# Whole-precision inverse products, DMA-transposed rows for the middle pairs, and the first norm's scaling at the end of beat 9

## The reference

```
u   = x @ in_proj_w.T + in_proj_b                # 512 -> 1536
uc  = short convolution of u, 3 taps, causal     # per channel, plus short_b
x0, x1, v = split(uc, 3)
k   = filter made by a small sine network, times a decay
v   = fftconv(v * x1, k) + bias * (v * x1)       # long causal convolution over 512 steps
x   = layernorm(x + (v * x0) @ out_proj_w.T + out_proj_b)
gate, up = x @ Wg.T, x @ Wu.T                    # 512 -> 1408; W = (codes - 128) * scale
x   = layernorm(x + (silu(gate) * up) @ Wd.T)
```

## Time and profile before

| | |
|---|---|
| median of 3 runs | 1064.79 us (1064.36 to 1066.73) |
| the profiled execution's own time | 1063.65 us |
| its span, first to last instruction | 1061.5 us |
| PE busy | 1023.4 us, 96% of the span, 6394 instructions |
| PEld busy | 831.9 us, 78% |
| DVE busy | 781.3 us, 74% |
| POOL busy | 639.2 us, 60% |
| ACT busy | 461.2 us, 43% |
| DMA queue q1, share of 16 engines | 27.2% |

### The profile page before, as it was taken

How to read it: one execution, slowest core, us unless ns; L and a number is a source line. 1 busy time by engine, 2 the same in 40 slices (tenths; PEclk the granted TensorE clock), 3 DMA queues, 4 the chain that set the end, 5 groups by cost and what they waited for, 6 DMA issues and landing times.

```text
span 1061.5 us, 18026 instructions
## 1 busy us (share of the span) xinstructions
PE 1023.4 (96%) x6394; PEld 831.9 (78%) x6394; DVE 781.3 (74%) x1416; ACT 461.2 (43%) x986; POOL 639.2 (60%) x685
## 2 busy tenths in 40 slices
PE   7998799999999999999999999999999999989996
PEld 5577678888888888888888888888888888868774
DVE  6577776877788787777878777787877778775554
ACT  4565344434454443444444444544435444424242
POOL 4578765675757567475756747575674756585210
PEclk9898899999999999999999999999999999999998
DMA  7565202222221312321122222312121212222232
GB/s 233 179 189 186 73 22 70 90 80 61 80 90 41 100 41 80 95 85 50 52 93 76 80 61 80 90 47 93 41 82 59 80 52 64 75 60 81 91 103 75
DMA packets 51783, 89.66 MB, mean 84 GB/s; under 512 B 6314, under 2 KB 11178, under 8 KB 51694
## 3 DMA queue, kind: packets, MB, share of 16 engines
q1 hardware_dynamic: 50930, 88.25, 27.2%
q10 hardware_dynamic: 764, 0.27, 0.1%
HBM read 77.22 MB, written 11.27 MB: 83 GB/s over the span
## 4 chain that ended last, share of the span: by engine, by line
PE 81%; DVE 7%; issue 4%; ACT 3%; POOL 2%; DMA 1%; ACTq 0%; SPq 0%; POOLq 0%; DVEq 0%
PE gate_up L995 12%; PE gate_up L996 12%; PE bank L852 10%; PE bank L854 10%; PE bank L853 10%; PE down L1006 7%; PE down L1007 7%; PE bank L956 3%; PE bank L978 1%; PE spectrum L852 1%; PE spectrum L854 1%; PE spectrum L853 1%; DVE tmp L755 1%; PE bank L909 1%; PE bank L957 1%
## 5 line engine op out<-in xcount | busy, mean ns | idle before, releaser
L602 ACT ACTIVATE hid<-gate_up,gate_scale 128x256 f32<-128x256 f32 x176 | 83.2, 473 | 208.3 <-PE gate_up L996 204.1
L755 DVE TENSOR_TENSOR tmp<-spectrum,filt 128x512 f32<-128x512 f32 x256 | 172.7, 679 | 0.0
L637 POOL TENSOR_TENSOR acc<-acc,tmp 128x256 f32<-128x256 f32 x160 | 124.4, 778 | 78.4 <-DVE tmp L755 68.1
L995 PE MATMUL gate_up<-x2T_hi,wg_sb 128*128 128x256 f16 x704 | 165.1, 275 | 0.0
L996 PE MATMUL gate_up<-x2T_lo,wu_sb 128*128 128x256 f16 x704 | 163.3, 273 | 0.0
L996 PE MATMUL gate_up<-x2T_lo,wg_sb 128*128 128x256 f16 x704 | 163.3, 273 | 0.0
L995 PE MATMUL gate_up<-x2T_hi,wu_sb 128*128 128x256 f16 x704 | 163.2, 273 | 0.0
L852 PE MATMUL bank<-xT_hi,win_hi 128*128 128x512 f32 x360 | 150.2, 417 | 2.9 <-POOL win_lo L620 1.7
L1006 PE MATMUL down<-wd_sb,hid_hi 128*128 128x512 f32 x352 | 147.8, 420 | 4.3 <-DVE hid_lo L842 2.2
L854 PE MATMUL bank<-xT_hi,win_lo 128*128 128x512 f32 x360 | 144.0, 400 | 0.0
L853 PE MATMUL bank<-xT_lo,win_hi 128*128 128x512 f32 x360 | 144.0, 400 | 0.0
(11 more groups left out here) (170 smaller groups left out, 2177.7 us busy)
## 6 DMA issues: line engine op xcount, KB each, us to landing
wd_sb<-wd_scratch SPq DMA_DIRECT2D x176, 256.0 KB, 2.6
xstage<-in_x SPq DMA_DIRECT2D x32, 256.0 KB, 4.3
x<-in_x SPq DMA_DIRECT2D x28, 256.0 KB, 2.7
out<-x SPq DMA_DIRECT2D x28, 256.0 KB, 3.3
x<-in_win SPq DMA_DIRECT2D x12, 256.0 KB, 4.8
acc<-in_decay SPq DMA_DIRECT2D x4, 256.0 KB
x<-in_wout SPq DMA_DIRECT2D x4, 256.0 KB, 2.8
x2T_hi<-in_wu SPq DMA_DIRECT2D x4, 256.0 KB, 4.1
```

Of the source, the lines that this page charges most:

```text
L637: G.tensor_tensor(acc[:, i, 0, :], acc[:, i, 0, :], t[:, 1, :], ALU.subtract)
L755: TT(dst, spectrum[j % 2][:, :, :], k_part, ALU.mult).then_inc(made_done, 1)
L995: mm(dst, w[:, kb, rows(q)], x2T_hi[:, kb, ts], start=kb == 0, stop=False)
```

## The change

It does four things.

1. All halves take the whole sums: `psplit`, `acc_hi`, `acc_lo`, `y_low`, `WHOLE` and `LIGHT` are gone, and `iv` is 4 calls of `matmul` on float32 for each of the four blocks of each half. `y` is one operation. The inverse matrix is no longer split, so one of 18 staged weights goes.
2. Pairs 1 to 12 (`BY_DMA`) have no `x2t` on PE. At the end of beat 10 ACT writes a float16 copy of each scaled row tile to `parts`, DVE writes the float16 rest, and SP issues four transposing DMAs (128x512 float16 each) to `x2T_hi` and `x2T_lo`. `gu` of unit 0 waits for all four. Pairs 0, 13, 14 and 15 keep `x2t`.
3. `norm` of LN1 stands at the end of beat 9 instead of near the start of beat 10.
4. `bank_read` becomes one semaphore for each bank, and an entry waits for the last read of its own bank.

```diff
-NFLOAT, NCODE, CODE_SLOTS = 18, 35, 5
+NFLOAT, NCODE, CODE_SLOTS, TEMPS = 17, 35, 5, 4
+BY_DMA = range(1, HALVES - 3)
-    if beat == 0 and 0 <= n - 3 < HALVES:
+    if beat == 0 and 0 <= n - 3 < HALVES and n - 3 not in BY_DMA:
         steps += [("x2t", n - 3, 0), ("x2t", n - 3, 1)]
-    if beat == 10 and out:
-        steps += [("norm", LN1, n - 2)]
+    if beat == 9 and out:
+        steps += [("norm", LN1, n - 2)]
     if beat in (9, 10):
         steps += readers([p for p in shared(n, beat) if p[0] == "xt"])
-    if beat in SPLIT_OF_BEAT and convs and n - 1 not in LIGHT:
-        steps += [("psplit", n - 1, SPLIT_OF_BEAT[beat])]
+    if beat == 10 and n - 2 in BY_DMA:
+        steps += [("x2part", n - 2, 0), ("x2part", n - 2, 1), ("x2dma", n - 2)]
...
+def by_dma(m):
+    return min(max(m - BY_DMA[0], 0), len(BY_DMA))
...
# SP
+elif kind == "x2dma":
+    m, = at
...
+    if m >= 2:
+        sp.wait_ge(gate_up_ready, HB * (m - 1))
+    for part, dst, done in ((0, x2T_hi, x2_hi_done), (1, x2T_lo, x2_lo_done)):
+        for b in range(2):
+            sp.wait_ge(done, 2 * (m if part == 0 else by_dma(m)) + b + 1)
+            sp.dma_start_transpose(dst[:, :, rows(pair_block(m, b))], parts[:, b, part, :]).then_inc(x2t_in, 16)
# ACT
+elif kind == "x2part":
+    m, b = at
+    act.wait_ge(ln_done[LN1], 2 * m + b + 1)
+    if m > BY_DMA[0]:
+        act.wait_ge(x2t_in, 64 * by_dma(m))
+    A(parts[:, b, 0, :], row_tile(m, b), ACT.Copy).then_inc(x2_hi_done, 1)
# DVE
+elif kind == "x2part":
+    m, b = at
+    dve.wait_ge(x2_hi_done, 2 * m + b + 1)
+    TT(parts[:, b, 1, :], row_tile(m, b), parts[:, b, 0, :], ALU.subtract).then_inc(x2_lo_done, 1)
# DVE, first product of a block
-                        if n - 1 in WHOLE:
+                        if n:
                             dve.wait_ge(bank_ready, use["iv", n - 1, i] + 1)
-                        elif n:
-                            dve.wait_ge(acc_lo_done, splits["psplit", n - 1, i] + 1)
# PE, iv
+                    pe.wait_ge(temp_added, temp["mul", n, i, i, 1] + 1)
+                    if k == use["iv", 0, 0]:
                         pe.wait_ge(inv_in, 16)
                     for c in range(2):
                         for r in range(2):
+                            last = mm(dst[:, rows(c)], acc[:, i, r, rows(c)], inv_sb[:, r, :], start=r == 0, stop=r == 1)
# PE, gu
-                    if q == 0:
-                        pe.wait_ge(bank_read, use["x2t", m, 1] + 1)
+                    if q == 0 and m in BY_DMA:
+                        pe.wait_ge(x2t_in, 64 * by_dma(m + 1))
+                    elif q == 0:
+                        pe.wait_ge(*read_of(use["x2t", m, 1]))
```

More of the change, by code:

```diff
@@ L203, in program @@
             now = beat_steps(n, beat)
-            at = next((k for k, s in enumerate(now) if s[0] in ("psplit", "mul")), len(now)) if n in (1, 2) else len(now)
+            at = next((k for k, s in enumerate(now) if s[0] == "mul"), len(now)) if n in (1, 2) else len(now)
             steps += now[:at] + setup_steps(n, beat) + now[at:]
@@ L257, in build @@
         acc = sb("acc", [P, TB, 2, W], F32)
-        acc_hi, acc_lo = (sb(f"acc_{n}", [P, 2, 2, W], F32R) for n in ("hi", "lo"))
-        tmp = sb("tmp", [P, 4, 2, W], F32)
+        tmp = sb("tmp", [P, TEMPS, 2, W], F32)
         za_hi, za_lo = (sb(f"za_{n}", [P, 2, L], F32R) for n in ("hi", "lo"))
@@ L264, in build @@
         hid = sb("hid", [P, 2, W], F32)
-        y_low = sb("y_low", [P, 2, P], F32)
+        parts = sb("parts", [P, 2, 2, D], F16)
         hid_hi, hid_lo = (sb(f"hid_{n}", [P, 2, W], F32R) for n in ("hi", "lo"))
@@ L295, in build @@
         gate_up_ready, down_done = sem("gate_up_ready"), sem("down_done")
-        bank_read, made_done = sem("bank_read"), sem("made_done")
+        bank_read, made_done = [sem(f"bank_read{n}") for n in range(4)], sem("made_done")
         temp_added = sem("temp_added")
@@ L367, in build, with last_use, read_of @@
         wide_ring = [bank[0][:, :], bank[1][:, :], flat(gate_up[0][:, :, :]), flat(gate_up[1][:, :, :])]
-        wide_uses = use["x2t", 0, 0] // 4 * 4
+        wide_uses = use["x2t", 0, 0]
+        bank_index = [k % 4 if k < wide_uses else (k - wide_uses) % 2 for k in range(len(use))]
         def bank_of(k):
-            return wide_ring[k % 4] if k < wide_uses else bank[k % 2][:, :]
+            return wide_ring[bank_index[k]]
+        def last_use(index, k):
+            return max((n for n in range(k) if bank_index[n] == index), default=None)
+        def read_of(k):
+            return bank_read[bank_index[k]], bank_index[:k + 1].count(bank_index[k])
         def row_tile(m, b):
@@ L377, in temp_of @@
         def temp_of(step):
-            return tmp[:, temp[step] % 4, :, :]
+            return tmp[:, temp[step] % TEMPS, :, :]
         def z_of(n, i):
@@ L467, in _ @@
                             load_down(n)
+                elif kind == "x2dma":
+                    m, = at
+                    if m == BY_DMA[0]:
+                        sp.wait_ge(code_done, NCODE)
+                        for n in range(CODE_SLOTS):
+                            sp.wait_ge(wd_saved[n], 16 * saves_before[n][NCODE])
+                    if m >= 2:
[4 more added lines that the diff above has]
+                            sp.dma_start_transpose(dst[:, :, rows(pair_block(m, b))], parts[:, b, part, :]).then_inc(x2t_in, 16)
                 elif kind == "store":
@@ L555, in _ @@
                     A(flat(vT_hi[:, 2 * jp:2 * jp + 2, :]), bank_of(k), ACT.Copy).then_inc(v_hi_done, 1)
[L556 to L561, removed]
                 elif kind == "z":
                     n, i = at
[L564 to L567, removed]
+                    act.wait_ge(*read_of(use["iv", n, i]))
                     s, h = n // 2, n % 2
@@ L760, in _ @@
                     dve.wait_ge(bank_ready, k + 1)
-                    dve.wait_ge(bank_read, use["ip", n, 1, X0] + 1)
+                    dve.wait_ge(*read_of(use["ip", n, 1, X0]))
                     y = cx0[:, 2 * h:2 * h + 2, rows(i)]
[L763 to L772, removed]
+                    sums = bank_of(k)[:, :W].rearrange("p (c t) -> p c t", c=2)
+                    TT(y, sums, y, ALU.mult).then_inc(bank_read[bank_index[k]], 1)
                 elif kind == "ln1":
@@ L828, in _ @@
                     ts = rows(pair_block(m, b))
[L829 removed]
+                    TT(x2T_lo[:, :, ts], src, x2T_hi[:, :, ts], ALU.subtract).then_inc(bank_read[bank_index[k]], 1)
+                elif kind == "x2part":
+                    m, b = at
+                    dve.wait_ge(x2_hi_done, 2 * m + b + 1)
+                    TT(parts[:, b, 1, :], row_tile(m, b), parts[:, b, 0, :], ALU.subtract).then_inc(x2_lo_done, 1)
                 elif kind == "hmul":
@@ L857, in free_bank @@
             def free_bank(k):
-                last = k - (4 if k < wide_uses + 2 else 2)
-                if last >= 0:
-                    pe.wait_ge(bank_read, last + 1)
+                last = last_use(bank_index[k], k)
+                if last is not None:
+                    pe.wait_ge(*read_of(last))
                 return bank_of(k)
@@ L937, in _ @@
                     dst = free_bank(k)
-                    if n in WHOLE:
+                    pe.wait_ge(temp_added, temp["mul", n, i, i, 1] + 1)
+                    if k == use["iv", 0, 0]:
                         pe.wait_ge(inv_in, 16)
[L940 to L944, removed]
-                    for c in range(2):
[L946 to L954, removed]
+                    for c in range(2):
                         for r in range(2):
-                            mm(both, acc_hi[:, i % 2, r, rows(c)], flat(inv_parts[:, r, :, :]), start=r == 0, stop=False)
-                            last = mm(high, acc_lo[:, i % 2, r, rows(c)], inv_parts[:, r, 0, :], start=False, stop=r == 1)
+                            last = mm(dst[:, rows(c)], acc[:, i, r, rows(c)], inv_sb[:, r, :], start=r == 0, stop=r == 1)
                     last.then_inc(bank_ready, 1)
```

51 lines of the change are left out of this document (18 added, 33 removed).

## The result

The changed kernel takes 1050.85 us at the median of 4 runs (1046.86 to 1053.16). The kernel before took 1065.76 us beside it (4 runs, 1064.36 to 1066.83). The ratio is 0.9857 [0.9821, 0.9893], so the change gains 14.9 us. The profiled execution took 1053.16 us with a span of 1051.4. The forecast of 1050.9 us was met almost to the tenth, but by luck and not by its own working: two of its terms were wrong and their errors nearly cancelled.

A forecast was written before the change was run, and what follows sets the result against it. PE was taken to bound steps 3 to 15, busy 778.91 of 780 us. Terms -10.4 + 2.1 - 1.9 - 3.4 - 0.3 = -13.9 us take 1063.65 to 1049.75, by the median 1050.9 us; range 1045 to 1072.

The forecast's parts named there:

- transposes gone from PE, DMAs in time: Pairs 1 to 12: PE saves 0.87 us a pair, -10.4 us; the DMAs land before gu of unit 0, 0 us.
- whole sums: middle halves: Halves 2 to 14: 52 iv on PE at 0.04 us more each, +2.1 us; work off other engines gains nothing.
- whole sums: half 15, step 16 and behind: Shorter iv of half 15, -1.9 us, and shorter PE waits in step 16, -3.4 us.
- start: Start of the kernel: one staged weight fewer, one operation less on ACT and POOL, -0.3 us.
- norm moved: Norm one beat sooner: same program in even steps, passes two xsplit on each engine in odd steps; 0 us.
- T: Time per transposing DMA if strictly one after another; in time under 2.0 us, taken as under 2 from its bytes.
- off the path here, as PE has no gap: Middle halves: work removed from ACT, POOL and DVE by whole sums gains nothing.
- In odd steps it passes two xsplit on each. 0 by itself: Moved norm in odd steps: goes ahead of two xsplit on DVE and on ACT, at a cost of 0.
- rival 1: Pairs' DMAs go one after another at 2.6 us, landing 2.3 us late in 12 pairs: +28 us, 1079 us; chance 0.13.
- rival 3: Transposing DMAs take 5.2 us each, landing 12.7 us late 12 times: +152, about 1203 us; chance 0.04.
- rival 2: T between 2.0 and 2.3, or less gain in step 16, or dearer whole iv: about 1057 us; chance 0.13.
- The fourth: Rival that the ends of steps give more, all bounds at their good end: -19.4, 1045.4 us; chance 0.04.

The follow-up runs named there:

- e3: On e1, x2t put back on PE for all 16 pairs, so no transposing DMAs: 1052.51 us, ratio 0.9882 to the kernel before.
- e1: The changed kernel with only norm of LN1 put back at the start of beat 10: 1041.75 us, ratio 0.9784 to the kernel before.
- e2: The kernel before with only norm of LN1 moved to the end of beat 9: 1074.09 us, ratio 1.0092.
- e4: On e1, each transposing DMA issued as two of half the size, eight per pair: 1101.92 us, ratio 1.0338 to the kernel before.
- e7: On e1, y is again three DVE operations, two of them useless: 1054.18 us, ratio 0.9906 to the kernel before.
- e5: On e1, pairs 13 and 14 also transposed by DMAs, four each: 1046.88 us, ratio 0.9832 to the kernel before.

## Why the forecast was right in the sum and wrong in two terms

| term | forecast | shown by the runs |
|---|---|---|
| transposes gone from PE, DMAs in time | -10.4 | -10.8 (e3 to e1) |
| whole sums: middle halves | +2.1 | -5.0 (by the marks, e3 against before; 1.3 of it also in e2) |
| whole sums: half 15, step 16 and behind | -5.3 | -6.0 (same) |
| start | -0.3 | not apart from the spread |
| norm moved | 0 | +9.1 (changed against e1), +9.2 (e2) |
| sum | -13.9 | -12.7 by these rows; -14.9 by the medians |

By its medians e3 gives 12.4 us for the two rows of whole sums that make 11.0 here; this and the spread between runs make up the difference of the two sums.

**Transposes and DMAs: right.** The 0.87 us a pair were there, and nothing took their place but one wait of 0.4 us (pair 6, whose last DMA landed after 4.5 us and not 2.6). The cause given was half right. The bytes, from which I argued that T would be under 2 us, do not matter; a price for each instruction on the queue does, and 1.26 us is under the limit of 2.0 us that I had worked out. The cover is thin: eight instructions overran it at once (e4). Neither figure of the Trainium skill that I had weighed tells the time here. The 1309 ns for a 128x128 transpose ("VectorE: DVE Perf Modes", three transpose paths), paid for each block in turn, would have made a DMA of four blocks 5.2 us by my estimate, and it lands in 2.6. By the 261 GB/s ("DMA: Bandwidth & Descriptors", latency and other measured facts) its 128 KB are 0.5 us by my estimate, and it holds SP for 1.26 us alone.

**Whole sums in the middle: the sign was wrong.** The step that failed is "off the path here, as PE has no gap". PE's row was read alone. DVE's `y` held banks that PE's weight loads wanted, and delayed `hid_lo`: 3.2 of the 5.0 us. e7, which changes nothing on PE, loses 3.6 us in the same two stretches and 8 to 12 in all. The other part, the price of `iv` itself, was mis-sized: I took 0.04 us more for each from an early whole `iv` that stands at 1.20 us to the second follower, and in the full stage it is 564.89 - 563.76 = 1.13 us, so 52 x 0.03 = -1.6 instead of +2.1. Whether ACT's and POOL's missing work, the semaphores by bank or the missing weight has a part in what is left was not tried apart.

**Half 15 and step 16: right.** `iv` takes 0.81 us (929.83 to 930.64 in beat 2 of step 16), where 0.89 was forecast. The wait for POOL's sum is 1.16 us where "under 1" was forecast, and 6.0 us came for 5.3. As forecast, what is late next is the same sum.

```profile
929.83 1.06 PE L944 MATMUL bank<-inv_sb,acc 128*128 128x128 f32 x8
930.64 0.48 PE L995 MATMUL down<-wd_sb,hid_hi 128*128 128x512 f32 x1
```

**The norm: wrong.** The sentence that failed is "In odd steps it passes two xsplit on each. 0 by itself". The entries passed were named and not priced. The two scalings delay `xsplit` by 1.43 us and the wait for the shift by 0.56 more, and PE's transposes in beat 10 need the banks that `xsplit` frees. The sum against PE's next need of the bank was not made; over the six odd steps the stretch from `gu` to these transposes grew by 7.9 us (7 of them are idle PE) and the one behind them by 1.3, changed against e1.

By the rivals: that the DMAs go one after another at 2.6 us (rival 1) is excluded, and rival 3 with it. None of rival 2's conditions came; part of the gain was lost at the norm, which no rival named. The fourth, 19.4 us by better ends of the ranges, is passed by e1's 23.2, but the gain stands mostly in other places, and the moved norm hid it. A forecast whose total is met says little about its terms: only e1 to e3 brought the two errors to light.

**Open.** What giving DVE its work back costs is 12.4 us by the medians and 7.8 by the spans. The profiled execution of e7, at 1050.29 us, is the shortest of its six, 3.9 under their median, and that of e1 is 0.8 over its own. Part of it is the start: after a wait of 2.3 us near 30 us the granted clock stays at 1.00 in this trace of e7, where it falls to 0.50 in that of e1. What the longer runs of e7 spend more, no trace shows.

## What to carry to other kernels

When PE is full, read the waits of its weight loads before calling another engine's work free: 2.2 and 1.3 us of them stood there, and the two stretches gave 3.2 us once DVE's work was gone. Giving DVE its operations back cost 8 to 12 us though no instruction of PE changed, more than those two stretches hold. When an entry is moved ahead in an engine's order, price each entry that it passes by its length plus its own wait, and follow the bank that the passed entry frees to PE's next need of it. Of several edits, run each alone even if the total meets the forecast; here one edit gave back 9 of 23 us, and leaving it out makes the best kernel of all, 1041.75 us.

## What of the hardware was not expected

- A transposing DMA holds SP's queue for 1.24 to 1.34 us at the median whatever its size (128x256, 128x512 and 128x1024 float16), where a plain load of the down weights (256 KB) holds it for 0.32 us. It lands 2.4, 2.6 to 2.8 and 3.3 us after its issue. What SP pays for here is the number of instructions and not the bytes.
- A wait of PE of some 2 to 4 us can cost 1.6 us or more on top, since the granted clock stands at 1.2 GHz for 3 us or longer behind it. It did behind ten of twelve waits in e4 (60 us lost for 40.4 us of waits), behind one of 3.08 us in e5 and behind one of 1.87 us in e7. The same wait of 2.3 us in step 16 is followed by 0.55 in e2 (958 to 961 us) and by 1.00 in the kernel before (949 to 952 us).
- The same start gives different times. Near 30 us PE stands still for some 2.3 us in all kernels. Behind it the granted clock stays at 1.00 in the traces of e2 and e7, and in the others it falls to 0.50 and comes back sooner or later; before, then changed:

```profile
40.00:44.00 4.00, 4.00 (x16) 2.81 (x15) 1.50 (x2) 1.94 (x5) 3.86 (x4) 1.00 0.31 107
```

```profile
40.00:44.00 4.00, 4.00 (x15) 3.21 (x14) 0.51 (x1) 1.78 (x4) 3.45 (x3) 0.77 0.98 298
```

  The first `x2t` stood at 122.8 to 128.0 us over the kernels. This may be much of the spread between runs of one kernel, 0.3 to 0.7%: among the last eleven runs of the kernel before, the shortest (1060.69 us) has a mean granted clock of 0.990 and the longest (1068.38 us) 0.981, and in every set of runs the time tends to fall as this clock rises. Where in the run the clock was lost, only the profiled executions show.
